# The last cross-attention of a four-layer block: the next stage's VectorE work cut into single operations, and each score matmul issued beside the transposed scores of the other head

## The reference

```
q, k, v = heads(LN(x) @ wq + bq), heads(ctx @ wk + bk), heads(ctx @ wv + bv)   # 16 heads of 8
logits = q @ k.T / sqrt(8) + temporal_bias
x = x + softmax(logits) @ v @ wo + bo
h = LN(x);  s = sigmoid(clip) * max|h| / 127;  hq = clip(round(h / s)) * s      # one maximum over all of h
w_gate, w_up, w_down -> rounded by the maximum of each row
x = x + w_down @ quant(silu(w_gate @ hq) * (w_up @ hq))
```

## Time and profile before

| | us |
|---|---|
| median of 3 runs | 1873.7 (1873.53 to 1874.37) |
| profiled execution: its time | 1879.15 |
| profiled execution: its span | 1876.9 |
| PE busy | 1645.0 (88%) |
| DVE busy | 1302.5 (69%) |
| ACT busy | 1053.6 (56%) |
| POOL busy | 550.5 (29%) |

### The profile page before, as it was taken

The page is one execution under the profiler, slowest core; times in us unless marked ns, Lnnn a source line. Parts: engine busy times, 40 slices in busy tenths (PEclk is TensorE's granted clock), DMA queues, the critical chain, the costliest instruction groups (busy, mean ns, idle before and its releaser), DMA issues. The chain is left out here.

```text
span 1876.9 us, 32707 instructions
## 1 busy us (share of the span) xinstructions
PE 1645.0 (88%) x11001; PEld 875.2 (47%) x11001; DVE 1302.5 (69%) x3515; ACT 1053.6 (56%) x2283; POOL 550.5 (29%) x634
## 2 busy tenths in 40 slices
PE   5877999996699999999999889988799886989974
PEld 3532333333455555555555456664566652333332
DVE  5536778857766666566666878856888666788747
ACT  2322666667554555555555368854588732666664
POOL 0316465510100000000000178814678304242200
PEclk9886999997799999999999989998899995999995
DMA  5214333201100000000000000001100002222100
GB/s 156 41 35 128 79 65 62 59 2 46 35 1 7 6 1 7 6 1 25 1 1 1 1 7 0 0 9 37 45 1 0 1 13 77 48 39 44 28 2 23
DMA packets 60239, 53.46 MB, mean 28 GB/s; under 512 B 9610, under 2 KB 52798, under 8 KB 59974
## 3 DMA queue, kind: packets, MB, share of 16 engines
q1 hardware_dynamic: 59238, 51.30, 11.5%
q10 hardware_dynamic: 864, 0.39, 0.1%
HBM read 30.57 MB, written 1.05 MB: 17 GB/s over the span
## 5 line engine op out<-in xcount | busy, mean ns | idle before, releaser
L1754 DVE CUSTOM_DVE_ANT_0 minus_s_l2x<-s_ps_l2x,mask_b_l2x 128x512 f32<-128x512 f32 x256 | 166.6, 688 | 183.2 <-PE s_ps_l2x L1970 183.2
L1879 ACT ACTIVATE probs_l2x<-minus_s_l2x,nmax_l2x 128x512 f32<-128x512 f32 x256 | 182.7, 714 | 187.2 <-DVE nmax_l2x L1754 187.1
L1060 DVE CUSTOM_DVE_ANT_0 junk_l1x<-s_ps_l1x,mask_b_l1x 128x512 f32<-128x512 f32 x256 | 166.3, 688 | 58.2 <-PE s_ps_l1x L1256 54.2
L1063 DVE TENSOR_REDUCE nmax_l3x<-s_ps_l3x 128x1 f32<-128x512 f32 x256 | 163.7, 684 | 50.5 <-PE s_ps_l3x L1256 48.4
L1122 ACT ACTIVATE pT_l1x<-st_ps_l1x 128x1024 f32<-128x1024 f32 x128 | 131.2, 1025 | 72.8 <-PE st_ps_l1x L1242 72.3
L1827 DVE COPY pT_l2x<-t_ps_l2x 128x512 f32<-128x512 f32 x256 | 164.3, 683 | 0.5 <-PE t_ps_l2x L1979 0.5
L1979 PEld LDWEIGHTS t_ps_l2x<-consts,probs_l2x 128*128 128x128 f32 x1024 | 109.6, 141 | 98.7 <-issue 87.2
L1979 PE MATMUL t_ps_l2x<-consts,probs_l2x 128*128 128x128 f32 x1024 | 139.8, 280 | 1.9 <-ACT probs_l2x L1879 1.9
L2560 POOL TENSOR_TENSOR rn_l2a_first<-ssc_l2a_first,consts 128x16 f32<-128x16 f32 x28 | 108.6, 3879 | 34.1 <-DVE ssc_l2a_first L2587 33.5
L2730 ACT ACTIVATE probs_l2a<-minus_s_l2a,nmax_l2a 128x128 f32<-128x128 f32 (+1 forms) x256 | 105.8, 417 | 10.3 <-DVE nmax_l2a L2635 9.0
L2635 DVE CUSTOM_DVE_ANT_0 minus_s_l2a<-s_ps_l2a,consts 128x128 f32<-128x128 f32 (+1 forms) x256 | 66.8, 316 | 52.6 <-PE s_ps_l2a L2845 47.8
(11 more groups left out here) (533 smaller groups left out, 3681.3 us busy)
## 6 DMA issues: line engine op xcount, KB each, us to landing
mask_i_l1x<-in_mask SPq DMA_DIRECT2D x8, 512.0 KB, 3.7
maskT_i_l1x<-in_mask_t SPq DMA_DIRECT2D x8, 512.0 KB, 4.9
kT_l1x_first<-parts_l1x_first SPq DMA_DIRECT2D x60, 64.0 KB
kT_l3x_first<-parts_l3x_first SPq DMA_DIRECT2D x60, 64.0 KB
q_l1x<-parts_l1x_first SPq DMA_DIRECT2D x90, 32.0 KB
q_l3x<-parts_l3x_first SPq DMA_DIRECT2D x90, 32.0 KB
ctxT_l0x<-in_ctxT SPq DMA_DIRECT2D x9, 256.0 KB, 3.2
rows_l0x<-in_ctx SPq DMA_DIRECT2D x9, 256.0 KB, 4.2
```

What stands on the lines that cost most here:

```text
L1060: dve.tensor_tensor_reduce(out=junk[w][:], in0=s_ps[w][:], in1=mask_b[b % 2][:, j, :], scale=-1.0, scalar=3e38, op0=ALU.add, op1=ALU.min, ...
L1063: dve.tensor_reduce(to, s_ps[w][:], AX.X, ALU.max, negate=True).then_inc(m.s_drained[w].sem, 1)
L1754: dve.tensor_tensor_reduce(out=minus_s[n % 4][:], in0=s_ps[n % 2][:], in1=mask_b[b % 2][:], scale=-1.0, scalar=3e38, op0=ALU.add, op1=ALU. ...
L1879: act.activation(probs[n % 4][:], minus_s[n % 4][:], ACT.Exp, bias=nmax[:, b % 2, n:n + 1], scale=-1.0, accum_out=sums[:, b % 2, j, h:h + ...
```

## The change

All edits act in `l3x` alone (the other caller of `pair_attention` has a mask, and keeps its order). PE's transposed scores are cut in two by head and interleaved with the scores: S0, transposed scores of head 1 (**T1**), S1, transposed scores of head 0 (**T0**). `FirstQuant.vector` does its operations one or two per step instead of all at offsets 0 and 6. The rounding of the weights is cut into 14 parts, spread over the first three batches. POOL's `power` gets another key in its sorted order.

```diff
-                    order += [(8 * b + 15, follow.power, (pool, b)) for b in range(B if biased else B - 1)]
+                    order += [(8 * b + 15.6, follow.power, (pool, b)) for b in range(B if biased else B - 1)]
...
-                def transposed_scores(t, j):
+                def transposed_scores(t, j, heads=(0, 1)):
                     b, p = divmod(t, PP)
-                    if t >= 1:
+                    if t >= 1 and heads[0] == FIRST_TURNED:
                         pe.wait_ge(*m.exp_done.after(2 * t + j - 1))
...
                     for e in range(2):
                         c = 2 * j + e
-                        for w in range(2):
+                        for w in heads:
...
-                    ins.then_inc(m.st_filled.sem, 1)
-
-                def scores(t, j):
+                    if len(heads) == 2 or heads[0] != FIRST_TURNED:
+                        ins.then_inc(m.st_filled.sem, 1)
+
+                def scores(t, j, heads=(0, 1)):
...
-                        if 0 <= t < T:
-                            transposed_scores(t, j)
-                        if t + LEAD < T:
-                            scores(t + LEAD, j)
+                        if masked:
...
+                        else:
+                            for w in range(2):
+                                if t + LEAD < T:
+                                    scores(t + LEAD, j, (w,))
+                                if 0 <= t < T:
+                                    transposed_scores(t, j, (1 - w,))
...
     def vector(self, dve, b, offset):
-        if offset == 0:
-            self.moments(dve, b)
-        if offset == 6:
-            self.scale(dve, b)
-        if b == 0 and offset in range(8, 16, 2):
-            self.weights(dve, offset // 2 - 4)
+        if offset in (0, 1):
+            dve.bn_stats(self.st[:, t0 + offset, :], x[:, t0 + offset, :]).then_inc(m.out_stats.sem, 1)
+        if offset == 2:
+            dve.wait_ge(*m.out_stats.after(t0 + TPB))
+            for t in range(t0, t0 + TPB):
+                dve.bn_aggr(self.mv[:, t, :], self.st[:, t, :]).then_inc(m.out_moments.sem, 1)
+        if offset == 3:
...
+            dve.tensor_scalar(self.ve[:, cols], self.mv[:, cols, 1], LN_EPS, None, ALU.add).then_inc(m.out_eps.sem, 1)
+        if offset in (6, 7):
...
+            dve.tensor_scalar(self.xn[:, t, :], x[:, t, :], self.mv[:, t, 0:1], self.rs[:, t:t + 1], ALU.subtract, ALU.mult)\
+                .then_inc(m.out_normed.sem, 1)
+        if offset == 8:
...
+            dve.tensor_reduce(self.peaks[:, b:b + 1], self.xn[:, cols, :].rearrange("p t d -> p (t d)"), AX.X, ALU.max,
+                              apply_absolute_value=True).then_inc(m.out_peaked.sem, 1)
+        if b < 3 and offset in (4, 5, 10, 12, 13):
+            self.weights(dve, 5 * b + (4, 5, 10, 12, 13).index(offset))
```

More of the change, by code:

```diff
@@ L780, in pair_attention @@
     LAST_SLOT = T + 5
+    FIRST_TURNED = 0 if masked else 1
     FOLLOWED = 28
@@ L1235, in transposed_scores @@
                                       start=True, stop=False)
-                    if j == 0 and p % 4 == 0:
+                    if j == 0 and p % 4 == 0 and heads[0] == FIRST_TURNED:
                         pe.wait_ge(*landed(m.max_moved, 2 * b + p // 4, 32))
@@ L1243, in transposed_scores @@
                                             start=not masked, stop=not masked or e == 1)
-                    ins.then_inc(m.st_filled.sem, 1)
-                def scores(t, j):
+                    if len(heads) == 2 or heads[0] != FIRST_TURNED:
+                        ins.then_inc(m.st_filled.sem, 1)
+                def scores(t, j, heads=(0, 1)):
                     b, p = divmod(t, PP)
-                    if p == 0 and j == 0:
+                    if p == 0 and j == 0 and heads[0] == 0:
                         pe.wait_ge(*stack_landed(b))
@@ L2023 @@
     NC, LAST = len(ROWS), ROWS[-1]
-    PARTS = 4
     def __init__(self, m):
@@ L2080, in weights @@
             dve.tensor_scalar(dscale, dscale, 1.0 / QMAX, None, ALU.mult).then_inc(step.sem, 1)
+        if part == 4:
             dve.wait_ge(*step.after(6))
@@ L2083, in weights @@
             dve.reciprocal(self.dinv, dscale).then_inc(step.sem, 1)
-        if part == 2:
-            dve.wait_ge(*step.after(8))
+        if 5 <= part < 5 + NC:
+            if part == 5:
+                dve.wait_ge(*step.after(8))
+            c = part - 5
             for n in range(2):
-                for c, r in enumerate(self.ROWS):
-                    dve.tensor_scalar(rows(n, c), rows(n, c), self.winv[0:r, n, c:c + 1], MAGIC, ALU.mult, ALU.add).then_inc(step.sem, 1)
+                r = self.ROWS[c]
+                dve.tensor_scalar(rows(n, c), rows(n, c), self.winv[0:r, n, c:c + 1], MAGIC, ALU.mult, ALU.add).then_inc(step.sem, 1)
+        if part == 5 + NC:
             dve.tensor_scalar(wd, wd, self.dinv, MAGIC, ALU.mult, ALU.add).then_inc(step.sem, 1)
-        if part == 3:
-            dve.wait_ge(*step.after(9 + 2 * NC))
+        if 6 + NC <= part < 6 + 2 * NC:
+            if part == 6 + NC:
+                dve.wait_ge(*step.after(9 + 2 * NC))
+            c = part - 6 - NC
             for n in range(2):
-                for c, r in enumerate(self.ROWS):
-                    dve.tensor_scalar(self.wq[0:r, n, c, :], rows(n, c), MAGIC, QMAX, ALU.subtract, ALU.min).then_inc(m.quant_ready.sem, 1)
+                r = self.ROWS[c]
+                dve.tensor_scalar(self.wq[0:r, n, c, :], rows(n, c), MAGIC, QMAX, ALU.subtract, ALU.min).then_inc(m.quant_ready.sem, 1)
+        if part == 6 + 2 * NC:
             dve.tensor_scalar(self.wdq, wd, MAGIC, QMAX, ALU.subtract, ALU.min).then_inc(m.quant_ready.sem, 1)
+        if part == 7 + 2 * NC:
             dve.tensor_scalar(self.diag, m.consts["ident"], dscale, None, ALU.mult).then_inc(m.quant_ready.sem, 1)
[L2098 to L2104, removed]
-            dve.bn_aggr(self.mv[:, t, :], self.st[:, t, :]).then_inc(m.out_moments.sem, 1)
-        dve.wait_ge(*m.out_moments.after(TPB * (b + 1)))
-        cols = slice(TPB * b, TPB * (b + 1))
-        dve.tensor_scalar(self.ve[:, cols], self.mv[:, cols, 1], LN_EPS, None, ALU.add).then_inc(m.out_eps.sem, 1)
     def power(self, pool, b):
```

24 lines of the change are left out of this document (14 added, 10 removed).

## The result

| | before | after |
|---|---|---|
| median | 1873.62 (1873.28 to 1874.37) | 1855.20 (1853.57 to 1855.61) |
| profiled execution: time | 1879.15 | 1855.61 |
| profiled execution: span | 1876.9 | 1853.4 |

The ratio of the runs is 0.990, with a 95% interval of 0.9882 to 0.9917. The forecast was 1860.1 with a range of 1853 to 1869. The sign and the range are right; the gain is 4.9 us larger than the 13.6 I had.

A forecast was written before the change was run, and what follows sets the result against it. PE and DVE were taken to hold each other up by turns, with transposed scores needlessly on the loop. Terms of 7.2 - 0.8 + 5.3 + 1.3 + 1.0, less 0.4, gave 13.6 us: median 1860.1, range 1853 to 1869.

The forecast's parts named there:

- PE's order: PE's loop in l3x: transposed scores done while S1 waits for DVE, 36 times 0.2, saving 7.2 us.
- Tail: Steps behind the last scores: heads no longer alternate, 0.33 in place of 0.23 in 14 steps, losing 0.8 us.
- Scalings: DVE's scalings and reduction in separate steps: 1.0 us in each of four batches, 0.9 in the fifth, saving 4.9.
- Statistics: DVE's statistics in steps of their own: 0.2 us saved in each of two batches.
- Rounding: DVE's rounding of the weights: blocks cost 2.4 us, spread parts 1.1, saving 1.3.
- Clock: Stretches at 1.2 GHz in the stage: PE pauses less with DVE's blocks cut, saving 1.0 us, bounds 0 and 5.
- Rival (d): The lower clock in the stage goes away altogether: 4 us more gained, 1856; chance 0.12 with anything lower.
- Overlap: Removing transposed scores from the loop and spreading DVE's work relieve some of the same waits: 0.4 us less gain.
- Rival (c): ACT becomes the loop: V waits 0.2 to 0.3 in each of 28 groups, up to 8 us, 1868; chance 0.11.

The follow-up runs named there:

- pe_only: The kernel before with only PE's order changed, FirstQuant and POOL's key left as before: 1867.59 us, ratio 0.9963.
- dve_only: The kernel before with only FirstQuant's operations spread and POOL's key changed, PE's loop as before: 1863.37 us, ratio 0.9937.
- tail_alt: The changed kernel, but behind the last scores the transposed matmuls alternate between the heads again: 1854.24 us, ratio 0.9896.
- same_head: The changed kernel with the heads of the transposed scores swapped (S0, T0, S1, T1): 1859.19 us, ratio 0.9928.
- weights_block: The changed kernel with the rounding of the weights in four blocks of the first batch, as before: 1858.54 us, ratio 0.9911.
- warm: The kernel before with 132 transposed-score matmuls added in 11 steps where PE pauses: 1870.23 us, ratio 0.9978.
- before_again: The kernel before, unchanged, profiled a second time: 1873.47 us.
- t_between: The changed kernel with all transposed scores issued between the two scores (S0, T1 and T0 by turns, S1): 1853.51 us.
- scale_block: The changed kernel with FirstQuant's two scalings and the reduction in one step again: 1862.64 us, ratio 0.9945.
- covered: The changed kernel with t_between's edit, the attention's own scalings split, and FirstQuant's operations moved behind long projections: 1853.89 us, ratio 0.9896.

## Why the prediction was right, and where 4.9 us came from

- **PE's order, 7.2.** Right, and on the low side. In the stage, with the clock taken off and the same way in, it is worth 8.1 with DVE's blocks in place (before to pe_only) and 8.7 with them cut (dve_only to tail_alt's stage). Raw medians say 8.2 for the latter (dve_only to changed), and 7.5 by each one's distance from before. So the term was 0.9 to 1.5 too small. "I round the 41 down to 36" and 0.2 for 0.23 would account for it, 41 x 0.23 = 9.4 being a little too much; no run tests the count by itself. That T must leave the loop, and not only its place, same_head shows: with the heads swapped 7.2 of the stage went back.
- **Tail, -0.8.** Wrong: nothing was lost. From the last four maxima to the last three exponentials it takes 17.6 with the old order (before, tail_alt) and 17.65 with the new.
- **Scalings, 4.9.** Right: 1.1 in each of three batches, 0.9 to 1.1 in the fourth, which has a stretch too, and 0.4 in the fifth: 4.6 to 4.8. A part of the working was wrong: of a pair only the first still meets POOL's splits, and the scalings' median fell from 0.56 to 0.34. The fear that they would grow past 0.83 had no ground.
- **Statistics, 0.4.** Not tested by themselves. Scalings and rounding make 7.2 to 7.4 together where DVE's whole order makes 6.8 to 7.3, so nothing is seen of this term.
- **Rounding, 1.3.** Too small, by an estimate that takes the clock's price off: 2.6 in the stage (weights_block less changed). Blocks cost 2.5 over a quiet batch in warm (32.0 to 29.5), where the forecast had 2.4. The spread parts, for which it had 1.1, can be read against weights_block, which has none: they cost 0.5 in the third batch, 0.2 in the fifth, -0.2 in the sixth, and 0.4 in the fourth, if a quiet one would take 27.3 there. That is 0.9. What the blocks cost beyond the 2.5 when T isn't in the loop was not tested further.
- **Clock, 1.0.** The main error. Medians give 3.3 (warm), the profiled run 6.0. The step that failed is "I take 1.0, since the quiet batch has the same block and no such stretch behind it": the last of the seven batches is quiet in before_again and not in before, with the same instructions. That a batch had no stretch was chance in that run and no proof that blocks are harmless. The prediction's own rows gave 2.7 for two of the three stretches, and its bound of 5 was closer than its choice. Rival (d), the lower clock gone altogether, had a chance of 0.12 and is what happened to the clock.
- **Overlap, -0.4.** None can be seen: in the stage 8.1 + 6.8 = 14.9 for the halves, against 230.4 - 215.0 = 15.4 for both.
- **Rival (c)**, ACT in the loop, is there only in traces: from 1600 to 1776 V waits nine times for an exponential, 2.3 us together, where before it was three times and 0.7, and once 0.2 for the copy. t_between has one such wait, and its stage is 0.2 shorter.

Against the 4.9: the clock gives 3.3 - 1.0 = 2.3 and the tail 0.8. The other terms made 13.4 in the forecast and 15.4 in the stage, 2.0 more, from PE's order and the rounding. That is 5.1, but it isn't an exact account: the 2.3 comes from medians, the 2.0 from profiled runs with priced stretches.

The three errors all made the forecast too small, and 1855.2 lies outside the 1857 to 1864 that had the chance of 0.50. By the time alone (d) with its 1856 would be the better forecast. The runs say that both its mechanisms, T off the loop and DVE's blocks cut up, work as described, and that the clock's part in what the blocks cost was underrated.

## What to carry to other kernels

Read a stretch's clock before its waits, and if the same pause is followed by a lower level in some repetitions only, don't price it by a quiet one; a second profile of the same kernel shows how much of it is chance, and matmuls added in the pauses show the cause. When two engines hold each other up by turns, list what stands between one's release and the other's start, and move what nobody there needs into a wait, not only to another place in the row: behind a late matmul on the same rows it is still on the loop. Work cut into single operations paid here (scale_block, weights_block). Moving it on into the idle behind long matmuls gained nothing more (covered): put in no more than the idle holds, each operation at its price beside whatever runs on POOL at that time.

## What the runs showed of the hardware

- **Two halves of the rows don't wait for each other.** In same_head S1 (rows 64 on) started at 1673.38 with S0, and the two T0 that were issued between them at 1673.60 or later. In t_between S1 started at 1674.52, and the last of T, issued ahead of it, at 1674.62. A row doesn't say which head a T belongs to, but all of them fit an order that is kept within each half. The Trainium skill, TensorE: Matmul & The Clock Gate (Part 3, The mechanism), says that matmuls start and end in the order of issue. The starts in these rows disagree, and the measurement decides; ends are modelled in the profile and settle nothing. V, which uses all rows, came behind both.
- **512 columns in one half beside twice 256 in the other** take 0.23 us from start to start (1608.72 to 1608.95), as equal ones do (1688.65 to 1688.88).
- **Single operations of VectorE slow down beside POOL.** A pair of 128x128 roundings took 0.35 alone and 1.44 beside a split of 1.35 on POOL, and a scaling 0.83 in place of 0.34.
- **A stretch at 1.2 GHz cost less than half its length**: 1.5 us for 3.4, 2.2 to 2.3 for 6.8. DVE's part of the loop doesn't slow down with PE (a maximum takes 0.67 to 0.69 in these stretches, as it does elsewhere), which would explain it; no run tests that.
